# Turns of the engines' streams in another order, with fewer clock products, in a two-layer decoder on one core

## The reference, cut to what matters

```python
x = x + _L0_attn_ref(_layernorm(x), Wq, bq, Wk, bk, Wv, bv, Wo, bo)    # 16 heads of 32, causal
x = x + _L0_xattn_ref(_layernorm(x), ctx_512, ctx_512)                 # 32 query heads, 8 key heads, no weights
x = x + _L0_ffn_ref(_layernorm(x), w_gate, w_up, w_down)               # silu(gate) * up, all operands block-quantised
x = x + _L1_attn_ref(_layernorm(x), Wx, Wg, bg, Wo, A, Dp)             # state space, below
x = x + _L1_xattn_ref(_layernorm(x), ctx_512, Wq, Wkv_expand, Wout)    # 16 heads, keys and values from the context
x = x + _L1_ffn_ref(_layernorm(x), W, gate_w, A, B)                    # x W' + low-rank experts, the best 2 of 8
```

## Time and profile before

| | us |
|---|---|
| median of 3 runs | 1565.12 (1564.77 to 1566.97) |
| profiled execution, own time | 1566.7 |
| its span | 1565.0 |
| TensorE busy | 1437.2 (92%) |
| VectorE busy | 1292.5 (83%) |
| ScalarE busy | 1034.5 (66%) |
| GpSimd busy | 430.5 (28%) |
| clock products L1926 | 142.8, 980 of them |
| granted clock, mean | 0.974 |

### The profile page before, as it was taken

One profiled execution on the slowest core, in us unless ns is written; L12 is line 12 of the kernel. 1 busy time (PEld: TensorE's weight loads), 2 busy tenths in 40 slices (PEclk: granted clock), 3 DMA queues, 4 the chain that ended last, 5 costly groups with the idle time before them and its releaser, 6 DMA issues.

```text
span 1565.0 us, 34443 instructions
## 1 busy us (share of the span) xinstructions
PE 1437.2 (92%) x13858; PEld 817.2 (52%) x13858; DVE 1292.5 (83%) x1969; ACT 1034.5 (66%) x1884; POOL 430.5 (28%) x519
## 2 busy tenths in 40 slices
PE   7898898989999999999999878889999999999997
PEld 5564545354455453554453445546556555565654
DVE  6999999989689788887797999878698888978743
ACT  3244365574773856665696779884899788979431
POOL 1532142232340422331331340151321313121310
PEclk9899989999999999999999999998999999999999
DMA  6313122200202012002220004101020210101020
GB/s 229 95 55 95 44 60 69 75 16 5 72 15 55 22 42 49 15 22 55 80 75 28 1 1 152 39 7 45 2 72 16 58 46 27 41 5 45 2 82 28
DMA packets 52943, 76.07 MB, mean 49 GB/s; under 512 B 7729, under 2 KB 22577, under 8 KB 52273
## 3 DMA queue, kind: packets, MB, share of 16 engines
q1 hardware_dynamic: 52784, 73.87, 16.6%
HBM read 38.98 MB, written 9.44 MB: 31 GB/s over the span
## 4 chain that ended last, share of the span: by engine, by line
PE 48%; DVE 30%; ACT 11%; issue 7%; POOL 3%; DMA 1%; SPq 0%; ACTq 0%; POOLq 0%; DVEq 0%
PE bank L203 16%; DVE mix_NM L1085 5%; PE bank L1196 5%; DVE ssm_HS L1555 3%; PE bank L998 2%; PE bank L539 2%; PE bank L1222 2%; PE bank L500 2%; PE bank L983 2%; PE bank L547 2%; PE bank L562 2%; ACT ssm_DA L1503 2%; ACT mix_P L1058 2%; PE bank L1926 1%; PE bank L527 1%
## 5 line engine op out<-in xcount | busy, mean ns | idle before, releaser
L1058 ACT ACTIVATE mix_P<-bank 128x512 f32<-128x512 f32 x256 | 142.5, 605 | 48.8 <-PE bank L983 48.3
L1085 DVE TENSOR_REDUCE mix_NM<-bank 128x2 f32<-128x512 f32 x256 | 162.5, 683 | 11.2 <-PE bank L958 10.6
L738 POOL TENSOR_SCALAR_AFFINE_SELECT cross_P<-cross_P 128x256 f32<-128x256 f32 x128 | 87.9, 697 | 272.0 <-ACT cross_P L647 272.0
L1555 DVE TENSOR_TENSOR_SCAN ssm_HS<-ssm_DA,ssm_DD 128x1024 f32<-128x1024 f32 x64 | 150.4, 2350 | 9.4 <-ACT ssm_DD L1506 5.7
L1314 POOL TENSOR_TENSOR ffn_room<-ffn_room 128x512 f32<-128x512 f32 x64 | 90.7, 1419 | 242.8 <-ACT ffn_room L1253 154.7
L738 POOL TENSOR_SCALAR_AFFINE_SELECT attn_P<-attn_P 128x256 f32<-128x256 f32 x128 | 82.7, 659 | 227.6 <-ACT attn_P L647 227.0
L1926 PE MATMUL bank<-ident 128*128 128x256 bf16 x980 | 142.8, 285 | 0.4 <-DVE XR L720 0.2
L1503 ACT ACTIVATE ssm_DA<-ssm_Z,A_T 128x255 f32<-128x255 f32 x256 | 110.9, 498 | 2.6 <-DVE ssm_HS L1555 2.3
L1926 PEld LDWEIGHTS bank<-ident 128*128 128x128 bf16 x980 | 93.0, 102 | 33.4 <-issue 16.7
L647 ACT ACTIVATE attn_P<-bank 128x384 f32<-128x384 f32 x128 | 64.2, 501 | 52.0 <-PE bank L528 51.6
L647 ACT ACTIVATE cross_P<-bank 128x384 f32<-128x384 f32 x128 | 62.4, 487 | 46.5 <-PE bank L528 46.3
(11 more groups left out here) (404 smaller groups left out, 4024.2 us busy)
## 6 DMA issues: line engine op xcount, KB each, us to landing
attn_stack<-attn_P SPq DMA_DIRECT2D x96, 128.0 KB, 2.5
cross_stack<-cross_P SPq DMA_DIRECT2D x96, 128.0 KB, 2.4
ffn_room<-f_gate SPq DMA_DIRECT2D x4, 1024.0 KB, 5.3
XR<-x SPq DMA_DIRECT2D x8, 512.0 KB, 6.6
ffn_room<-f_up SPq DMA_DIRECT2D x4, 1024.0 KB, 5.7
ffn_room<-f_down SPq DMA_DIRECT2D x4, 1024.0 KB, 5.3
x_mid<-XR SPq DMA_DIRECT2D x8, 512.0 KB, 3.1
XR<-x_mid SPq DMA_DIRECT2D x8, 512.0 KB, 3.8
```

The source lines that it names most:

```text
L738: nc.gpsimd.affine_select(out=diagonal, in_=diagonal, compare_op=ALU.is_ge, fill=0.0, base=0, pattern=[[0, 2], [1, P]], channel_multiplier ...
L1058: nc.scalar.activation(self.p[h % 8], bank[b4[h % 2]][:, :], ACT.Exp, scale=HD2 ** -0.5).then_inc(s["p_ready"], 1)
L1085: nc.vector.tensor_reduce(self.nm[:, t, 16 * i + 2 * g:16 * i + 2 * g + 2], bank[b4[u % 3]][:, :].rearrange("p (c k) -> p c k", c=2), AX.X ...
L1555: nc.vector.tensor_tensor_scan(flat(self.hs), flat(self.da), flat(self.dd), 0.0, ALU.mult, ALU.add).then_inc(s["hs_ready"], 1)
```

## The change

The strings of `TURNS0` are written anew for all five engines. Each holds the same turns as before, but for the clock turns: 73 of j and 106 of k stay, 67 turns with 268 products are left out. The mean turn moves by less than one place on each engine (0.95 on SyncE, 0.87 on TensorE, 0.79 on ScalarE, 0.53 on VectorE, 0.73 on GpSimd), the farthest on TensorE by 21. And the value of `mixing_over` goes from B (8) to DC * B (32). The diff, with one line of each of two tables for the rest:

```diff
 TURNS0 = {
...
     "dve": (
-        "daggppbbgggpgppggggggggbbbbbbbbbbbbgggggggaggggbgbbbbgggbbabbcgggdggggdggbbbbbbbbbbbbdddgddgggdd"
+        "ggggggpagpdppbbpgggggggbbbbbbbbbbbbgaggggggggggbgbbbbgggbbabbcggggggdggdgbbbbbbbbbbbbdddgddddggd"
...
-        mixing_over = (mix.s["x_done"], B)
+        mixing_over = (mix.s["x_done"], DC * B)
...
-                             in_turn(lambda i: keep_clock(pe, banks, 5, i), 85),
-                             in_turn(lambda i: keep_clock(pe, banks, 2, i), 161))
+                             in_turn(lambda i: keep_clock(pe, banks, 5, i), 73),
+                             in_turn(lambda i: keep_clock(pe, banks, 2, i), 106))
```

More of the change, by code:

```diff
@@ new lines @@
+        "hhhehfhhiehehhffeheifhehihhefhefhghhhehehghhhghehhhheehegeghhgegeiehhhhhehhhfehhiehhhhhhhhehhhhh"
+        "hhhehhhehhehfeheiehehfehifhihhfhhfhehfhhhfhghihhghhgihgghhgghhhhhhhhkhhiikhhhhhhhhhihhhhhhhhhhhh"
+        "hihikhihihkhihkhihhhkhihihhhkhkhkhhhikhihhihhhhhhhhiikkikkikkiikkkkkikiikii"),
+    "act": (
+        "jjjbajaajaaaaaaaaaadadaaaaaaaaaaadaaaaaaaaadaaaaadabaaaabaabaddaabbbbbaaaaaaaadaaaaaaaaaaaadaaaa"
+        "aaaaadaaaabaaabbddbbabbbbaababaababbadbbabaababbadabaabababbaababbbdbbbbbabbabbadbbbbbaabbabaaaa"
+        "aaaadadbbbbbabbbbababababbabbadabbadaaababbbababbaabbadaadbbbabbbbabbbababbbaabbbdbdcaaaacacccba"
+        "acccaccccaaccbbbcbbbcbcbbcbabccbbbacabbacababccabababbbaaabcbcacbabccbacbcaacbacbbabbcabbcbcaabc"
+        "acbbbcacbbbcbccaacaaaccaabacaaaccacccbcccbbbbcbbabbcbbcabbbacbbacabbaabbaccabbbaaabbccabbabbacbb"
+        "baacabbaabbbacbaabbbabbcbbcaacaabacaacccaacacacbcacbbcbbbbcbbcbbcbbbcbbcbbbbcbbcbbbcbbabbcbbbbbb"
+        "bcbbacabcabbacbababbaaccacaacacaaacaacacaaccbaabcabbcbbcbbcbbabbcabbbcbcbbccbbbabbbcbbbababbbbba"
+        "bbabbabababbaabbbbbabaacaaacaacaaaaacacaacacaaacabcccacbabbbbcbbbcbbcbbbbbkbbkcbbcbbbebbkbbekbbc"
+        "ebbbcbbkbbkbcbccbebbecbbbbeeeeeceeeecebeeeeeceeccccecbcccbbcbbbbcbbbbcbbbcbbcbbcbbcbbbbbcbbcbbcc"
+        "bbbbbbbcbefcfecfcfffcccceffccffcfffecfccfcffcecffcfceeeceecceeceefecefcfcfffeefeeegffflffglfgfee"
+        "eleelfffflfleefffeehhehffffhffhfheheeheehffffefghefhhghfhhhfhghfhfhhfheehhfhhfhfhheehefhfhffffhe"
+        "hhfhfheihhihhfiheeehehhghhiehehhihhheehhghhhfhgfhhfeehfffhheeeffhhhfeehhiiehehihhefffffeehefehfi"
+        "heffheheehehfhfihfhfhhefhehfhhheehgfhfheegefeehgefhffhfffffeehhheefefhhhihifhhefeefifhfffefhffhe"
+        "hfhehhehhehhhgihhhhhhiehhgehgeeheeheeffffffffefeheheheefihfhehhihhfffeeifehffhfehfhfehfheheehfhh"
+        "hihfhhfhehhihehhgeehegeffgehhfeeefffffefeehhheeffhfhihhhhffifeeiefffffhfffefhehheheheghhhhheihgh"
+        "hhhhehghheeffhehfeeheeiffehhhfeefhhfhfhhhffeieeefheeffhfefhfhffhfhfhffhfhhhhhghehhhihghhghhhihhh"
+        "hhihhhihhhhihhihhhihhhhhhihhhhhhihhhiiiii"),
@@ L94 @@
+        "dhhhddgddddddfddddfhhhddddfhhffchdghhhhhhdedddhdfdhdddhdfdddhdddcfffdghhhehchhhffhfffdgdddddddhd"
+        "ddddhdddhhhhfhfhefdffdgdddddddddddddhddhhhiefjhhjhffffhghhhhfhhhfhffgkkhhhhhjhhhmlnnnnnnnnjnnnnn"
+        "nnnkmonnnnnnnnnnnnnnnnmkojnnnnnnnnnnjnnnnnnmonnnnnnnnnnnknnnnnjmonnnnnnnnnnnnknnnnjmonknnnnnnnnn"
         "nnnnnnmonnnnnnnnknnnnnnnnmonnnnnnnnnnnnnnnno"),
```

96 lines of the change are left out of this document (36 added, 60 removed).

## The result

The change makes the kernel 50 us faster: a median of 1515.43 us (1512.86 to 1518.33, 4 runs) against 1565.42 for the kernel before, a ratio of 0.968 (95% interval 0.966 to 0.970). Forecast were 1558.6 us in a range of 1549 to 1568.5. The direction was right, the size was an eighth of what came. The profiled execution of the change has a span of 1511.1 us, 53.9 less than before.

A forecast was written before the change was run, and what follows sets the result against it. VectorE bounds to 400 us and from 850 to 1050, TensorE from 400 to 850 and 1050 to 1500. Terms -5.0 - 4.0 - 0.5 + 1.5 + 1.5 = -6.5 us gave 1558.6 us, range 1549 to 1568.5.

The forecast's parts named there:

- The start: First row: VectorE begins at 6.2 us instead of 13.74, a transpose wait goes; 5.0 us gain (3.9 to 6.4).
- The order between the start and the last stage: 400 to 850 us: other turns move under one turn in the mean, no one direction seen; no gain counted.
- Same work, so nothing: VectorE's low halves of cross and final weights, spread among scans: no effect unless the stacks' clearing is late.
- The clock products of the last stage: 1050 to 1500 us: 26 of 28 turns left out; 4 us gain, 1.5 of it direct, bounds 1.5 to 11.3.
- waits that get filled: Last stage: other work fills some 6 of 24 waits where clock products stood; 2.5 us gain.
- Where TensorE waits for VectorE: nothing: First 100 us and around 900 to 1000: leaving out about 12 and some 15 clock turns gains nothing.
- The clock: TensorE's score phases without clock products: one more fall to half clock, 1.5 us loss.
- rival 3: Last stage: clock falls in scores that had clock products among them; slower, 1568 to 1580 us; chance 0.15.
- Table loads: ScalarE, near 1045 and 1290 us: four more, 63 in all, each 1.28 us; 1.5 us loss taken.
- Clearing of the stacks: Before the cross scores: clearing ends near 1005 us, 3 us left; if late, 1562 to 1568 us; chance 0.07.
- costs nothing: First scan waits for all of the mixing instead of a quarter, through mixing_over at 32: no loss.

The follow-up runs named there:

- new_start: Kernel before, with the change's turns for what ran in its first 100 us: 1559.97 us, ratio 0.996.
- new_100_460: Kernel before, with the change's turns for what ran from 100 to 460 us: 1543.14 us, ratio 0.986.
- order_alone: The change's order of all other turns, with all 246 clock turns of the kernel before at their old places: 1543.15 us, ratio 0.987.
- new_850_1060: Kernel before, with the change's turns for what ran from 850 to 1060 us: 1554.72 us, ratio 0.994.
- before_less_1080: Kernel before, less 27 clock turns (108 products) of 1080 to 1470 us: 1564.37 us, ratio 1.0004.
- change_plus_1080: The change, with 27 clock turns of 1080 to 1470 us put back where they stood in the kernel before: 1517.01 us.
- clock_products_out: Old order of all other turns, with the change's 179 clock turns at the change's places: 1575.27 us, ratio 1.0072 against the kernel before.
- clock_in_scores: Kernel before, plus 16 clock turns inside four runs of score products between 100 and 400 us: 1570.79 us, ratio 1.0033.
- less_100_400: The change without its 39 clock turns (156 products) of 100 to 400 us: 1525.66 us.

## Why the prediction was wrong

- **The start: right.** 5.0 us forecast, 5.2 measured at row 0, 5.4 in new_start's median. Within it, two sizes were off and cancelled, which is luck: unit 1's maximum came at 38.9 and not at 37.2, a gain of 2.2 instead of 3.9, and behind it 3.0 more came where I had 1.1 (5.0 less 3.9). My 6.2 for VectorE's first step was 6.31.
- **The order between the start and the last stage: the step that failed.** I wrote that the order of 400 to 850 had "moved by less than one turn in the mean, and I see no one direction in it", and gave 100 to 400 no term at all. new_100_460 measured 21 us for it (16.9 of 20.5 in order_alone's window, with before's clock turns), and new_850_1060 10 for the passage. The room was in my own rows: 28 us of VectorE's 41.84 idle in the first 400 were no initial wait, and I called them "a few". 19 of them are 23 waits for TensorE, none over 2.5 us. I had also counted the clock turns as removed and never looked where the 179 that are left would stand: the change's clock turns alone cost 10 us, and with the new order they gave 28.
- **"Same work, so nothing", for the spread low halves: failed.** Their place was a cover for clock products of TensorE. The passage gained 7.7 us up to scan 21 in new_850_1060, and nothing in order_alone, where before's clock turns stood among them. I had read the run of clock products beside them as harmless, which it was there, and not asked what the time was for.
- **The clock products of the last stage: right in kind.** I had 1.5 us direct and up to 11.3; before_less_1080 gave none, with a mean clock of 0.972 against 0.975 beside it, 9 us more at half, which at 0.24 each hides about 2 us (an estimate). So the reading that most stood in waits held. The 2.5 us for waits that get filled no run shows as such: change_plus_1080 puts the products back for 1.6 in the new order, and the whole stage gained 8.8 from scan 21 on where I had 4. "Where TensorE waits for VectorE: nothing" had the wrong sign for the first 430 us of before's order: clock_products_out was 14.0 us behind there, with 15 clock turns fewer, most of them in the first 100 us, the others at new places, and 88.7 us at half clock against 47.6.
- **The clock: wrong in sign for the change.** I expected one stretch more at half clock. The trace of the change has 58.2 us at half against 83.8 before, with 9 stretches for 15 (the short one in the last microseconds counted in both). Before's order with the change's clock turns did become slower, with 128.7 us at half, but not by rival 3's mechanism: from scan 21 to the last it had 13.6 us at half against 17.0. Of the 45 us more at half clock 41 came before 430 us.
- **Table loads:** 63, as read from the order; with a gain of 8.8 us from scan 21 to the last I can't say that they cost anything. It wasn't tried apart.
- **Clearing of the stacks:** the memsets end at 961.6 in the change and the first cross maximum is at 964.34, so 2.7 us of slack are left, where I had 3, and nothing waited. The rival was 3 us off coming true.
- **mixing_over:** the wait is now live, 2.37 us of ScalarE at 845.21 for GpSimd's last addition. The lead is 35.5 us at the feed-forward's row 5 (796 us), 34.7 at its row 6 and 34.8 at the first scan, so it cost little, if anything. In before's order, before_less_1080 carries the value 32 and is 0.6 us ahead at the first scan: nothing there. In new_850_1060 the same wait is as long, and 1.7 us are lost between row 5 and row 6. The new order with the value 8 wasn't tried, so "costs nothing" stays unproven for it.

What stays open: how much of the 21 us in 100 to 460 is the clock's. At the price of clock_products_out (12.6 us for 31 more at half) it would be 8, but there the places had changed too; at that of one kernel's executions (0.24) it would be 5; clock_in_scores removed 17 us at half up to unit 9 and had 0.3 to show, products paid. So most of the 21 is the order's waits, by these estimates. Both engines wait for each other there, and I found no kernel that changes the one alone. Open too is which waits the turns behind 1060 us remove.

## What to carry to other kernels

When two engines are each 90% busy in one stage and wait for each other in pieces of a microsecond, count those pieces as the room of a new order, and put that room into the range, even if each turn moves by one place. Cost filler work by the wait in which it stands, and ask after each reordering whether that wait is still there: the same exchange of clock turns, 67 fewer and the rest placed anew, was worth +10 us in one order and -28 in the other. When a run takes filler out, say whether what is left has moved, and count it in each stretch: here that tells a missing product from a misplaced one. And test a splice by stretches of time: here the products' parts added within 3 us (16.1 + 13.1 + 1.6 by places, 27.7 at once), which tells in a few runs where a gain is made.

## What the runs showed that I had not expected

- An advance of 4.7 us at 101 us and 5.2 at 418 is still 5.2 at 1452 us (new_start): the stages in which TensorE is the busier engine took nothing of it.
- The order of the other turns and the places of the clock turns move the clock, and not only the number of clock products. In the traces the mean clock is 0.981 in the new order with all 246 clock turns and with 179 alike, 0.974 in before's with its own 246, and 0.960 in before's with the change's 179 at the change's places. In the stretch to the feed-forward's row 0, 170 products at other places than before's 178 went with twice the time at half clock (61.4 us for 30.6).
- The worth of a stretch at half clock isn't one number: 31 us more went with 12.6 in before's order, 34 us more with 7.6 in the change's (less_100_400, 41.0 us at half between 100 and 400 against 6.8), where 156 products also left the list, and repeated executions of the one kernel before give 0.24 us for each.
